# Experts that gather their rows from token order, and attention openings written out by hand

## The reference

```
x = x + xattn0(layernorm(x), ctx);  x = x + ffn0(layernorm(x))        # ffn0: quantised, gated
x = x + xattn1(layernorm(x), ctx);  x = x + moe(layernorm(x))         # 16 heads, 64 keys per sample

def moe(x):                                                           # 8 experts, 2 for each token
    scores = x @ Wr + br
    _, topk_idx = top_k(scores, 2)
    indicator = one_hot(topk_idx, 8).sum(-2)
    weights = softmax(where(indicator > 0, scores, -inf))
    for i in range(8):
        h = relu((x * indicator[..., i:i+1]) @ W1[i] + b1[i])         # 256 -> 1024
        out += (h @ W2[i] + b2[i]) * weights[..., i:i+1]              # 1024 -> 256
    return out
```

## Time and profile before

| | us |
|---|---|
| median of 3 runs | 1434.64 |
| lowest, highest | 1417.69, 1437.44 |
| the profiled execution's own time | 1434.98 |
| its span in the trace | 1433.2 |
| PE busy, share of the span | 1231.8, 86% |
| DVE | 1025.3, 72% |
| ACT | 802.4, 56% |
| POOL | 522.3, 36% |

### The profile page before, as it was taken

How to read it: one execution, slowest core, us unless ns; L and a number is a source line. 1 busy time by engine, 2 the same in 40 slices (tenths; PEclk the granted TensorE clock), 3 DMA queues, 4 the chain that set the end, 5 groups by cost and what they waited for, 6 DMA issues and landing times. The chain is left out here.

```text
span 1433.2 us, 28369 instructions
## 1 busy us (share of the span) xinstructions
PE 1231.8 (86%) x8633; PEld 930.1 (65%) x8634; DVE 1025.3 (72%) x2058; ACT 802.4 (56%) x1212; POOL 522.3 (36%) x423
## 2 busy tenths in 40 slices
PE   8959999976999594997999998741799999999995
PEld 4526777763433283784677676741689889998874
DVE  3759999877989686676788988766465665666543
ACT  2545665564679787636788876650333443344341
POOL 2027777720000000001887875576033223232322
PEclk9989999999999656999999999555899999999998
DMA  6020000000024675101132232565223232223210
GB/s 225 1 70 1 1 0 0 0 1 1 0 89 176 236 238 176 72 1 48 37 128 88 88 117 74 172 202 180 68 52 48 44 55 45 46 45 53 47 29 7
DMA packets 61447, 106.06 MB, mean 74 GB/s; under 512 B 7488, under 2 KB 48704, under 8 KB 60736
## 3 DMA queue, kind: packets, MB, share of 16 engines
q1 hardware_dynamic: 48080, 88.24, 19.2%
q0 software_dynamic: 13296, 16.92, 6.3%
HBM read 66.96 MB, written 39.10 MB: 74 GB/s over the span
## 5 line engine op out<-in xcount | busy, mean ns | idle before, releaser
L2308 POOL DMA_INDIRECT out<-ex_yo,ex_mt x71 | 115.4, 1625 | 314.4 <-DVE ex_yo L2283 170.9
L2217 ACT ACTIVATE ex_hT<-ex_ps_h,e_b1T,e_unscale 128x256 f32<-128x256 f32 (+1 forms) x312 | 143.9, 545 | 113.3 <-PE ex_ps_h L2174 113.3
L2174 PE MATMUL ex_ps_h<-ex_xT_hi,a_arena 128*128 128x256 f16 (+1 forms) x1248 | 203.5, 265 | 0.3 <-issue 0.2
L607 PE MATMUL at_ps_y<-c_VW,at_pT_hi 128*128 (+1 forms) x1024 | 171.1, 273 | 3.5 <-DVE main_x_res L740 3.5
L927 POOL TENSOR_TENSOR at_sc<-at_sc,at_ri 128x960 f32<-128x960 f32 (+1 forms) x96 | 145.2, 1527 | 68.7 <-DVE at_ri L735 68.0
L2174 PE MATMUL ex_ps_h<-ex_xT_lo,a_arena 128*128 128x256 f16 (+1 forms) x624 | 164.5, 264 | 0.0
L585 PE MATMUL at_ps_s<-a_arena,at_xnT_hi 128*128 (+1 forms) x512 | 158.8, 393 | 4.3 <-issue 4.3
L2187 PE MATMUL ex_ps_y<-a_arena,ex_hT_hi 128*128 x568 | 154.9, 273 | 4.7 <-DVE ex_hT_lo L2265 4.1
L2187 PE MATMUL ex_ps_y<-e_w_lo,ex_hT_hi 128*128 x568 | 154.9, 273 | 0.0
L2187 PE MATMUL ex_ps_y<-a_arena,ex_hT_lo 128*128 x568 | 154.8, 273 | 0.0
L927 POOL TENSOR_TENSOR at_sc<-at_sc,at_mx 128x960 f32<-128x960 f32 (+1 forms) x96 | 134.1, 1411 | 26.0 <-DVE at_mx L712 25.9
(11 more groups left out here) (350 smaller groups left out, 2811.0 us busy)
## 6 DMA issues: line engine op xcount, KB each, us to landing
at_half<-in_L_ffn_W SPq DMA_DIRECT2D x32, 512.0 KB, 4.0
up_scratch<-gm_stg SPq DMA_DIRECT2D x16, 768.0 KB, 3.2
gm_stg<-up_scratch SPq DMA_DIRECT2D x16, 768.0 KB, 4.3
ex_row<-xs SPq DMA_DIRECT2D x32, 260.0 KB, 3.0
rt_stage<-in_L_ffn_W SPq DMA_DIRECT2D x16, 512.0 KB, 5.4
main_x_res<-in_x SPq DMA_DIRECT2D x8, 512.0 KB, 12.1
out<-main_x_res SPq DMA_DIRECT2D x8, 512.0 KB, 6.3
xs<-rt_pad SPq DMA_DIRECT2D x18, 130.0 KB, 2.4
```

Of the source, the lines that this page charges most:

```text
L607: last = nc.tensor.matmul(ps_y[:, 0:D], a[j][:, n, :], b[:, bass.ds(off + n * D, D)], start=(n == 0 and i == 0), stop=(n == NP - 1 and i = ...
L2174: last = nc.tensor.matmul(ps_h[:, n, at], a[:, bass.ds(e * WN + d * HID + n * P, P)], b[:, d, at], start=(m == 0), stop=(m == 3 * DT - 1))
L2217: last = nc.scalar.activation(hT[:, n, at], ps_h[:, n, at], ACT.Relu, bias=b1T[:, bass.ds(e * HT + n, 1)], scale=unscale[:, 0, bass.ds(e, 1)])
L2308: nc.gpsimd.indirect_dma_start(out=acc[:, :], out_offset=bass.IndirectOffsetOnAxis(ap=mt[j][:, q, 1:2].bitcast(U32), axis=0), in_=yo[j][:, ...
```

## The change

Three things change together.

In both attentions the first steps are written out: ACT normalises one tile further ahead in every step, and an Exp on one number comes before the first scores are copied; POOL's `add_bias` stands behind its other operations, for tile k + 2 instead of k + 4; `levels` comes three steps later. PE's order is the same. On ACT, at the opening of attention 0 (L633, in the new numbering L632, is the norm; L644 or L643 the copy of scores), there stands before:

The diff, cut:

```diff
...
-def in_steps_by(eng, n, lead, lag, u, step):
-
-    for k in range(-lead, u):
+def in_steps_by(eng, n, lag, u, step, tail=1):
+
+    for k in range(u):
         step(k, k % u)
-    with eng.Fori(1, n // u - 1, 1) as i:
+    with eng.Fori(1, n // u - tail, 1) as i:
         for j in range(u):
             step(u * i + j, j)
-    for k in range(n - u, n + lag):
+    for k in range(n - tail * u, n + lag):
...
+            turn_x(0, 0)
+            for t in range(3):
+                turn_x(t + 1, (t + 1) % 2)
+                scores(t, t % 2)
+            in_steps_by(nc.tensor, NT, 1, NS, step)
...
-                if there(k + 4, NT):
-                    norm(k + 4, j % 2)
-                if opening(k):
-                    high_x(k + 4, j % 2)
+                if there(k + 5, NT):
+                    norm(k + 5, (j + 1) % 2)
...
+            norm(0, 0)
+            norm(1, 1)
+            high_x(0, 0)
+            norm(2, 0)
+            high_x(1, 1)
+            norm(3, 1)
+            nc.scalar.activation(warm[:, :], unscale[:, 0:1], ACT.Exp)
+            take_scores(0, 0)
+            high_x(2, 0)
+            norm(4, 0)
+            take_scores(1, 1)
+            high_x(3, 1)
+            exps(0, 0)
+            take_scores(2, 2)
+            exps(1, 1)
+            in_steps_by(nc.scalar, NT, 0, NS, step, tail=2)
...
-                if quant and -2 <= k < 30:
-                    levels(k)
+                if quant and 0 < k <= NT:
+                    levels(k - 3)
...
-                if there(k + 4, NT):
-                    add_bias(k + 4)
+                if there(k + 2, NT):
+                    add_bias(k + 2)
...
+            subtract(0, 0)
             pool.wait_ge(bias_s, 16)
-            in_steps_by(nc.gpsimd, NT, 4, 0, NS, step)
+            add_bias(0)
+            subtract(1, 1)
+            normalise(0, 0)
+            subtract(2, 2)
+            add_bias(1)
+            in_steps_by(nc.gpsimd, NT, 0, NS, step)
...
-    NB = 4
+    NB = 3
...
-            for q in range(NS, 2 * E):
-                load_half(q)
             sp.wait_ge(cst, CONSTS)
-            for q in range(TR // P):
-                sp.dma_start(xs[E * CAP + q * P:E * CAP + (q + 1) * P, :], pad[:, :]).then_inc(padded, 16)
-            sp.wait_ge(cnt_r, 1)
-            for e in range(E):
-                n = nc.sync.value_load(cnt[0:1, e:e + 1], min_val=0, max_val=T)
-                for q in range(TR // P):
-                    sp.dma_start(xs[bass.ds(n + (e * CAP + q * P), P), :], pad[:, :]).then_inc(padded, 16)
-            sp.wait_ge(padded, 16 * (E + 1) * (TR // P))
+            sp.dma_start(xs[0:P, :], pad[:, :]).then_inc(padded, 16)
+            for c in range(NK):
+                sp.wait_ge(xn_r, TK * (c + 1))
+                sp.wait_ge(pay_r, c + 1)
+                sp.dma_start(xs[(TK * c + 1) * P:(TK * (c + 1) + 1) * P, :].rearrange("(i p) d -> p i d", p=P), pay[c % NB][:, :, :]
+                             ).then_inc(sent[c % NB], 16)
+                for q in range(NS + highs_to(c), min(NS + highs_to(c + 1), 2 * E)):
+                    load_half(q)
+            for j in range(NB):
+                sp.wait_ge(sent[j], 16 * len(range(j, NK, NB)))
+            sp.wait_ge(padded, 16)
...
-            for t in range(NT):
-                c, i = divmod(t, TK)
-                pool.wait_ge(meta_r, c + 1)
-                for k in range(2):
-                    g.indirect_dma_start(out=xs[:, :], out_offset=bass.IndirectOffsetOnAxis(ap=pos[c % NB][:, i, k:k + 1], axis=0),
-                                         in_=pay[c % NB][:, i, :], in_offset=None, bounds_check=last_row,
-                                         oob_is_err=True).then_inc(sent[t % (NB * TK)], 16)
-            for j in range(NB * TK):
-                pool.wait_ge(sent[j], 32 * len(range(j, NT, NB * TK)))
+            for c in range(NK):
+                mine = slice(TK * c, TK * c + TK)
+                out = pay[c % NB]
+                pool.wait_ge(oh_r, c + 1)
+                g.tensor_tensor(ind[:, mine, :], oh[:, 0, mine, :], oh[:, 1, mine, :], ALU.add).then_inc(ind_r, 1)
+                need(pool, sent[c % NB], 16 * (c // NB))
+                g.tensor_copy(out[:, :, D], idf[:, :, 0])
+                g.tensor_copy(out[:, :, D + 3].bitcast(I32), tok[:, mine].bitcast(I32))
+                pool.wait_ge(inv_r, c + 1)
+                g.tensor_tensor(out[:, :, D + 2], wt[:, 1, :], wt[:, 2, :], ALU.mult).then_inc(both_r, 1)
+                pool.wait_ge(both_r, c + 1)
+                g.tensor_tensor(out[:, :, D + 1], wt[:, 2, :], out[:, :, D + 2], ALU.subtract).then_inc(pay_r, 1)
+            for n in range(NG):
+                pool.wait_ge(spot_r, n + 1)
+                need(pool, slot_mm, n - 1)
+                t0 = GR * n % NT
+                g.tensor_tensor(in_slot[n % 2][:, 0, :, :], is_slot[n % 2],
+                                turn_no[:, t0:t0 + GR].unsqueeze(2).to_broadcast([P, GR, SLOTS]), ALU.mult).then_inc(turn_r, 1)
...
+            def rank():
+                pe.wait_ge(ind_r, NK)
+                pe.wait_ge(b1_c, 1)
+                pe.wait_ge(bmr_r, 1)
+                nc.tensor.matmul(ps_c[1][:, 0:NT * E], ones[:, :], ind[:, :, :], start=True, stop=True).then_inc(rank_mm, 1)
+                nc.tensor.matmul(ps_c[0][:, 0:NT * E], tri[:, :], ind[:, :, :], start=True, stop=True).then_inc(rank_mm, 1)
+
+            def to_slots(g):
+
+                pe.wait_ge(lane_r, g + 1)
+                pe.wait_ge(turn_r, g + 1)
+                pe.wait_ge(slot_r, g + 1)
+                for i in range(GR):
+                    last = nc.tensor.matmul(ps_i[:, 0:2 * SLOTS], in_lane[:, GR * g + i, :], in_slot[g % 2][:, :, i, :],
+                                            start=(g == 0 and i == 0), stop=(g == NG - 1 and i == GR - 1))
+                last.then_inc(slot_mm, 1)
...
+            for g in range(NG):
+                to_slots(g)
...
             ratio(NK - 1)
+            for g in range(NG):
+                act.wait_ge(spot_r, g + 1)
+                need(act, slot_mm, g - 1)
+                nc.scalar.activation(in_slot[g % 2][:, 1, :, :], is_slot[g % 2], ACT.Copy, scale=lane[:, 0:1]).then_inc(slot_r, 1)
...
+            def spread(g):
+
+                mine = slice(GR * g, GR * g + GR)
+                need(dve, slot_r, g - 1)
+                need(dve, turn_r, g - 1)
+                v.tensor_tensor(is_slot[g % 2], line[:, 0:SLOTS].unsqueeze(1).to_broadcast([P, GR, SLOTS]),
+                                part_f[:, 1, mine].unsqueeze(2).to_broadcast([P, GR, SLOTS]), ALU.is_equal).then_inc(spot_r, 1)
+                v.tensor_tensor(in_lane[:, mine, :], line[:, :].unsqueeze(1).to_broadcast([P, GR, P]),
+                                part_f[:, 0, mine].unsqueeze(2).to_broadcast([P, GR, P]), ALU.is_equal).then_inc(lane_r, 1)
+
+            for g in range(NG):
+                spread(g)
...
-        row = [s.sb(f"row{j}", [P, Q, ROW]) for j in range(2)]
+        RB = 4
+        row = [x_res[:, E:, :].rearrange("p t d -> p (t d)")[:, j * Q * ROW:(j + 1) * Q * ROW].rearrange("p (q d) -> p q d", q=Q)
+               for j in range(RB)]
...
-            def load(i, j):
-                rows = TR if not mixed(i) else P
-                need(sp, t_r, i - 1)
-                need(sp, meta_r, i - 1)
-                for n, q0, q1 in runs(i):
-                    r = look_up(nc.sync, 0, n, E * CAP // rows)
-                    sp.dma_start(row[j][:, q0:q1, :], xs[bass.ds(r * rows, rows), :].rearrange("(q p) d -> p q d", p=P)
-                                 ).then_inc(row_in[j], 16)
-
-            def step(k, j):
-                if there(k + 3, NTL):
-                    load(k + 3, (j + 1) % 2)
-
-            load(0, 0)
             sp.dma_start(b2s, b2.unsqueeze(0).to_broadcast([P, E, D])).then_inc(b2_in, 16)
-            in_pairs(nc.sync, 2, 0, step)
...
                 if there(k + 2, NTL):
-                    turn_x(k + 2, j)
+                    turn_x(k + 2, (j + 2) % RB)
                 if there(k + 1, NTL):
                     up(k + 1, (j + 1) % 2)
                 if there(k, NTL):
-                    down(k, j)
-
-            in_pairs(nc.tensor, 2, 0, step)
+                    down(k, j % 2)
+
+            in_fours(nc.tensor, 2, 0, step)
...
+            def fetch(i, q):
+
+                need(pool, t_r, i - RB + 1)
+                need(pool, meta_r, i - RB + 1)
+                n = 2 * i + q
+                nc.gpsimd.indirect_dma_start(out=row[i % RB][:, q, :], out_offset=None, in_=xs[:, :],
+                                             in_offset=bass.IndirectOffsetOnAxis(ap=slot[:, n:n + 1].bitcast(U32), axis=0),
+                                             bounds_check=last_sent, oob_is_err=True).then_inc(row_in[i % RB], 16)
+
+            def add(i, q):
                 pool.wait_ge(yo_r, i + 1)
-                for q in range(rows_of(i).stop):
-                    need(pool, added, 16 * (Q * i + q))
```

(23 more changed lines are left out.)

255 lines of the change are left out of this document (131 added, 124 removed).

## The result

The change makes the kernel slower: 1522.84 us median of 4 runs (1516.93 to 1539.18) against 1426.16 of 4 (1415.17 to 1437.44), a ratio of 1.0724 with a 95% interval of 1.0581 to 1.0866. The forecast was 1570, slower, with a range of 1506 to 1618.

What follows compares the result with a forecast made beforehand. PE alone was taken to set the pace in the experts' whole tiles. From 1434.98 us, -18 for the openings, +10 for the route and +143 for the experts gave 1570 us, range 1506 to 1618.

Steps and rivals of the forecast that it cites:

- The mechanism in the experts: Experts: POOL's last gather stands behind the second add, a loop of one tile, 15.67 instead of 10.92 us a step, +143.
- the two mixed intervals: Experts: the two intervals between turns among mixed tiles go from 15.12 us to 15.67, 0.8 us in all.
- turn to yo: Experts, in the step: from PE's turn of a tile until yo is done, 3.98 us.
- yo to add: Experts, in the step: from yo done to the start of POOL's first add, 0.8 us.
- add to add: Experts, in the step: from POOL's first add to its second, which waits for the first to land, 5.3 us.
- gather and landing: Experts, in the step: the last gather's issue of 0.97 us on POOL and its landing of 2.7.
- (a): Rival, experts: the fetches are hidden and the change does what its openings give, 1427 us, not slower; chance 0.07.
- (c): Rival, experts: the same loop but with its quickest terms, 14.2 us a step, 1525 us; chance 0.2.
- (d): Rival, experts: the loop, with PE's turn and the steps behind it slower, 17.0 us a step, 1609 us; chance 0.15.
- The openings: Start of both attentions: PE's holes go as ACT's norm is written one tile ahead, -18 us (-14 to -21).
- The route: Between attention 1 and the experts: scatters and pad transfers removed, new work behind the last chunk, +10 us (-6 to +15).
- spread: Route: four groups of DVE and POOL work, one after the other by the shared port rule, 23.7 us.

Runs made afterwards that it cites:

- the kernel with both gathers in front: The changed kernel with POOL issuing both gathers of tile k + 3 ahead of the two adds of tile k - 1; measured 1400.84 us.

## Why the prediction was right, point by point

**The mechanism in the experts.** It went as the prediction said, and moving four instructions undoes it. The size was 124.4 us instead of 143: a step is 14.90 us and not 15.67, so 30 steps give 119.5 instead of 142.5, and the two mixed intervals 3.0 (16.04 and 17.49 against 15.12 and 15.46) instead of 0.8. The terms of the step, as predicted and in the step from 1128.04 to 1142.20: turn to yo 3.98, measured 3.77; yo to add 0.8, 0.88; add to add 5.3, 4.73; the second add 1.62, 1.59; gap 0.30, 0.30; gather and landing 0.97 + 2.7, 2.89 in all. The sum of the measured ones is 14.16, which is that step. The term that was most off is the last: the landing of a transfer, in the trace's own summary, starts with the issue; further up it is said to start at the issue's end, and so the prediction added the two (in its bounds for the adds too). The step shows it: from the gather's start at 1139.31, an issue of 1.06 us and a landing of 2.8 behind it would end at 1143.17, and its rows are used at 1142.20. The summary for the gathers has 2.8 to 4.3, with 3.0 in the middle:

```profile
L2366 POOL DMA_INDIRECT main_x_res<-xs,e_slot x71: 1007/1061/1829, 969.2 to 1464.7; - x71
...
DMA to landing us min/median/max: 2.8/3.0/4.3
```

The mean step is longer than 14.16 in part because some of the issues are: 1.81 us instead of 1.06 for a gather, in a step of 15.33 us (1156.35 to 1171.68).

**The rivals.** (a), fetches hidden, is what the kernel with both gathers in front does, and near the price that (a) gave: 1427 less the 18 us of the first stage is 1409, measured 1400.84. (c), the shorter loop of 14.2, has the length of the quickest steps (nine of the 30 take 14.0 to 14.2), and its time of 1525 lies 2 us from the measured one. That is chance, since its sum too starts from the long first stage: from the short one it gives 1507 and the forecast 1552, and the measured time lies between the two, as the step of 14.90 does between 14.2 and 15.67. (The range, 18.3 us lower, would be 1488 to 1600 and hold it still.) (d) expected a slower clock, and it came, 0.93 over the stretch. PE's work stayed inside the step, but the steps were not alike: in 14 of the 30 the granted clock was 0.96 to 1.00 and they took 14.4 us in the mean, in the other 16 it was 0.82 to 0.90 and they took 15.3. In 13 of these 16 the last gather's issue was stretched (1.32 to 1.81 us), in none of the 14; whether the clock lengthens the step or the longer waits bring down the clock is not shown. PE is busy for 82% of the stretch and not 70, because the steps are shorter than was forecast (in the step at 1128.04, at a clock of 1.00, for 11.31 of 14.16 us) and because the same work takes longer at the lower clock (in that at 1156.35, at 0.89, 12.97 of 15.33).

**The openings.** -20.0 us (11.0 and 9.0), forecast -18. Holes of up to 1.20 us are left, a little more than the 1 us that was forecast.

**The route.** +2.5 to the first turn, forecast +10, which lies in its range of -6 to +15; the other profiles with the new route and POOL's products have 116.1 to 118.7, so +2 to +5. Step by step, from the route's start: last chunk 72 us (forecast 77), chain on DVE 9.8 (10.5), spread 19.5 (23.7), the rest 7.1 (5.4). A group of the spread takes 5.34 us and not 5.92, its operations being shorter than was taken, and POOL's last product falls into the rest, where the table's first comparisons end only behind it.

**The base.** The sum started from an execution with a first stage of 85.0 us; the median of after comes from ones with 66.7. Of the 46 us between the forecast and the profiled execution after (1523.74) that is 18.3; 18.6 are the experts' terms, 7.5 the route, 2 the openings.

## What to carry to other kernels

As POOL's rows show, a transfer that an engine issues in program order starts no sooner than what stands ahead of it there (the last gather 0.30 us behind the second add), so its lead is to be counted from the last wait ahead of it in that queue, not from the number of buffers. To find such a loop, follow one tile round: what releases the transfer, what releases that, until the same tile or its neighbour comes again; the length of the round over the number of tiles in it is a bound on the step, and either an earlier place in the queue (122 us here) or a lead of one more tile (119) takes it away. Of a change with several parts, each is to be measured alone: here one part gave 20 us and was hidden under another's 124.
